# A selective scan with six of sixteen states turned by diagonal matrices, four in-place state buffers, and scans of two channel groups at once

## The reference

```
x = x + mixer(ctx, layernorm(x))      # the gate z is layernorm(x)
x = x + ffn(layernorm(x))
# the mixer's core: for each batch b, channel e (512) and state n (16), over time l (512)
dA[l]    = exp(delta[e, l] * A[e, n])
state[l] = state[l-1] * dA[l] + (delta * u)[e, l] * B[n, l]
y[e, l] += state[l] * C[n, l]         # summed over the 16 states
y = (y + D * u) * silu(z)
```

## Time and profile before

| | |
|---|---|
| median of 3 runs | 699.42 us (696.72 to 703.13) |
| the profiled execution | 699.17 us, span 697.4 us |
| scan stage, first scan to last scan | 159.3 to 487.2 us |
| feed-forward network's first matmul | 494.0 us |
| busy, whole span | PE 553.5, DVE 548.0, ACT 565.9, POOL 490.5 us |

### The profile page before, as it was taken

The page is one execution under the profiler, slowest core; times in us unless marked ns, Lnnn a source line. Parts: engine busy times, 40 slices in busy tenths (PEclk is TensorE's granted clock), DMA queues, the critical chain, the costliest instruction groups (busy, mean ns, idle before and its releaser), DMA issues.

```text
span 697.4 us, 10143 instructions
## 1 busy us (share of the span) xinstructions
PE 553.5 (79%) x3560; PEld 391.0 (56%) x3560; DVE 548.0 (79%) x815; ACT 565.9 (81%) x769; POOL 490.5 (70%) x253
## 2 busy tenths in 40 slices
PE   5877788116897778877897776868889999999975
PEld 2433335116786768776786776866345454545442
DVE  3972262548999999999999999999499898988761
ACT  3873636759999999999999997977378898989773
POOL 2999255006999989999999986889455656555561
PEclk9988657557999999999999998899899999999999
DMA  8900090930121136221722228121300000000000
GB/s 281 361 1 0 0 344 25 382 129 31 48 60 54 53 84 189 61 62 57 207 72 60 59 53 267 47 56 37 60 1 16 31 26 22 30 16 31 16 31 30
DMA packets 25076, 59.16 MB, mean 85 GB/s; under 512 B 5105, under 2 KB 5105, under 8 KB 23362
## 3 DMA queue, kind: packets, MB, share of 16 engines
q1 hardware_dynamic: 22914, 54.32, 22.9%
q0 software_dynamic: 2112, 4.19, 3.5%
HBM read 47.89 MB, written 10.62 MB: 84 GB/s over the span
## 4 chain that ended last, share of the span: by engine, by line
ACT 44%; PE 36%; DVE 8%; POOL 5%; issue 4%; DMA 3%; POOLq 0%; DVEq 0%; SPq 0%; ACTq 0%
ACT arena L506 19%; ACT arena L510 19%; PE ps L942 15%; PE ps L957 6%; ACT arena L453 3%; PE ps L797 3%; PE ps L779 3%; PE ps L885 2%; DVE arena L640 2%; DVE arena L571 2%; POOL arena L321 2%; PE ps L896 2%; PE ps L949 2%; DMA arena<-w_all 1%; DMA arena<-ctx_t 1%
## 5 line engine op out<-in xcount | busy, mean ns | idle before, releaser
L354 POOL TENSOR_TENSOR arena<-arena 128x1024 f32<-128x1024 f32 x128 | 300.4, 2388 | 68.1 <-DVE arena L640 55.4
L640 DVE TENSOR_TENSOR_SCAN arena<-arena,ps 128x512 f32<-128x512 f32 x256 | 290.2, 1199 | 22.1 <-PE ps L885 16.6
L885 PE MATMUL ps<-ident,arena 128*128 128x128 f32 x1024 | 161.8, 283 | 76.0 <-ACT arena L506 63.0
L885 PEld LDWEIGHTS ps<-ident,arena 128*128 128x128 f32 x1024 | 121.3, 145 | 91.0 <-ACT arena L506 68.5
L506 ACT ACTIVATE arena<-arena,bT 128x512 f32<-128x512 f32 x256 | 162.9, 706 | 4.7 <-DMA w_ternary<-arena 4.7
L896 PE MATMUL ps<-ident,arena 128*128 128x128 f32 x1024 | 158.9, 278 | 8.1 <-DVE arena L647 4.7
L510 ACT ACTIVATE arena<-arena,a_neg 128x512 f32<-128x512 f32 x256 | 163.2, 707 | 0.1
L896 PEld LDWEIGHTS ps<-ident,arena 128*128 128x128 f32 x1024 | 123.0, 143 | 11.1 <-POOL arena L354 4.8
L942 PE MATMUL ps<-arena 128*128 128x512 bf16 x512 | 120.9, 386 | 4.8 <-DVE arena L724 2.6
L382 POOL TENSOR_TENSOR arena<-arena 128x1024 f32<-128x1024 f32 x32 | 75.4, 2355 | 26.6 <-DVE arena L724 26.6
L942 PEld LDWEIGHTS ps<-arena 128*128 128x128 bf16 x512 | 49.3, 99 | 61.0 <-issue 8.6
(11 more groups left out here) (90 smaller groups left out, 641.7 us busy)
## 6 DMA issues: line engine op xcount, KB each, us to landing
arena<-c_rows SPq DMA_DIRECT2D x64, 256.0 KB, 3.2
arena<-w_all SPq DMA_DIRECT2D x12, 1024.0 KB, 9.5
w_ternary<-arena SPq DMA_DIRECT2D x12, 512.0 KB, 7.7
arena<-w_ternary SPq DMA_DIRECT2D x3, 2048.0 KB, 10.1
arena<-x SPq DMA_DIRECT2D x4, 1024.0 KB, 8.1
arena<-x POOLq DMA_DIRECT2D x4, 1024.0 KB, 12.4
out<-arena SPq DMA_DIRECT2D x16, 256.0 KB, 2.0
arena<-ctx_t SPq DMA_DIRECT2D x2, 1024.0 KB, 8.5
```

The lines of the kernel that those rows point to most:

```text
L354: nc.gpsimd.tensor_tensor(ps_[:, s, 2 * half:2 * half + 2, :], hs[:, s, 2 * half:2 * half + 2, :], c_bc[:, s:s + 1, :].to_broadcast([P, 2, ...
L640: nc.vector.tensor_tensor_scan(out=hs[:, s, i, :], data0=dA[:, s, i, :], data1=ps[:, 4 + i, :], initial=0.0, op0=ALU.mult, op1=ALU.add).th ...
L885: last = nc.tensor.transpose(ps[:, 4 + i, c * P:(c + 1) * P], dB[:, s, c, i * P:(i + 1) * P], ident[:])
```

## The change

- In states n = 1, 3, 9, 11, 13 and 15 (24 of 64 values of k) ACT no longer scales `turned` into `dB`. It scales the 128x128 identity by the column B[n] into `dgB`, four instructions of 128x128, and TensorE multiplies `turned` itself by this diagonal matrix: four real float32 matmuls of 128x128 for each group instead of four transposes. `dB` and `dgB` have two buffers each, by order of use.
- `hs` has four buffers (`RING`), and the product is written in place over the state; `ps_` is gone. `product(k)` is one instruction of 128x2048 after all of scan k, where it was two of 128x1024.
- A scan covers two groups, 128x1024. The carry from one group to the next is cut by a zero in column 0 of `dA`: one memset before the first scan sets it, and L510's exponentials write columns 1 to 511 only. VectorE waits, as ACT does, until the ternary weights are stored, since `dA` lies over their staging.
- TensorE's stream goes by halves (two groups) and adds one state later; `gate_y` moves from n = 1 to n = 2.
- `xn` and `q1` move, and have one place for the early tiles and one for the later ones.

The diff, cut to what acts in the scan stage:

```diff
+RING = 4
+DIAG = (1, 3, 9, 11, 13, 15)
...
-        hs = part(128, 16).rearrange("p (s k l) -> p s k l", s=2, k=KE)
-        ps_ = part(144, 16).rearrange("p (s k l) -> p s k l", s=2, k=KE)
+        dgB = part(198, 4).rearrange("p (s k e) -> p s k e", s=2, k=KL)
+        hs = part(128, 32).rearrange("p (s k l) -> p s k l", s=RING, k=KE)
         c_bc = part(160, 4).rearrange("p (s l) -> p s l", s=2)
         skip = part(196, 2).rearrange("p (k e) -> p k e", k=KE)
-        q1 = part(198, 3).bitcast(BF16).rearrange("p (s n) -> p s n", s=EARLY)
-        xn = part(201, 2)
+        xn_early = part(72, 2)
+        q1_early = part(74, 3).bitcast(BF16).rearrange("p (s n) -> p s n", s=EARLY)
...
+        def is_diag(k):
+            return k % DS in DIAG
+
+        def slot(k):
+
+            return len([j for j in range(k) if is_diag(j) == is_diag(k)]) % 2
+
+        def slot_free(k):
+
+            same = [j for j in range(k) if is_diag(j) == is_diag(k)]
+            return same[-2] * KE + KE if len(same) > 1 else 0
...
-                hold(sp, "p_ready", (k - 2) * 2 + 2)
+                hold(sp, "p_ready", k - 1)
...
             def product(k):
                 s = k % 2
                 pool.wait_ge(c_loaded[s], (k // 2 + 1) * 16)
-                for half in range(2):
-                    hold(pool, "scan_done", k * KE + 2 * half + 2, *added(k - 2, half))
-                    nc.gpsimd.tensor_tensor(
-                        ps_[:, s, 2 * half:2 * half + 2, :], hs[:, s, 2 * half:2 * half + 2, :],
-                        c_bc[:, s:s + 1, :].to_broadcast([P, 2, L]), ALU.mult).then_inc(S["p_ready"], 1)
+                pool.wait_ge(S["scan_done"], k * 2 + 2)
+                nc.gpsimd.tensor_tensor(hs[:, k % RING, :, :], hs[:, k % RING, :, :],
+                                        c_bc[:, s:s + 1, :].to_broadcast([P, KE, L]),
+                                        ALU.mult).then_inc(S["p_ready"], 1)
...
-                    hold(act, "dBu_ready", (k - 2) * KE + KE)
+                    hold(act, "dBu_ready", slot_free(k))
                     for i in range(KL):
-                        nc.scalar.activation(dB[:, s, i, :], turned[:, b, i, :], ACT.Copy,
-                                             scale=bT[:, b, i, n:n + 1]).then_inc(S["dB_ready"], 1)
+                        if is_diag(k):
+                            nc.scalar.activation(dgB[:, slot(k), i, :], ident[:], ACT.Copy,
+                                                 scale=bT[:, b, i, n:n + 1]).then_inc(S["dB_ready"], 1)
+                        else:
+                            nc.scalar.activation(dB[:, slot(k), i, :], turned[:, b, i, :], ACT.Copy,
+                                                 scale=bT[:, b, i, n:n + 1]).then_inc(S["dB_ready"], 1)
                     for i in range(KE):
-                        hold(act, "scan_done", (k - 2) * KE + i + 1)
-                        nc.scalar.activation(dA[:, s, i, :], delta_u[:, b, 0, i, :], ACT.Exp,
+                        hold(act, "scan_done", (k - 2) * 2 + i // 2 + 1)
+                        nc.scalar.activation(dA[:, s, i, 1:], delta_u[:, b, 0, i, 1:], ACT.Exp,
                                              scale=a_neg[:, i, n:n + 1]).then_inc(S["dA_ready"], 1)
...
             def scan(k):
-                b, s = k // DS, k % 2
-                for i in range(KE):
-                    hold(dve, "p_ready", (k - 2) * 2 + i // 2 + 1)
-                    dve.wait_ge(S["dA_ready"], k * KE + i + 1)
-                    dve.wait_ge(S["dBu_ready"], k * KE + i + 1)
-                    nc.vector.tensor_tensor_scan(out=hs[:, s, i, :], data0=dA[:, s, i, :], data1=ps[:, 4 + i, :],
-                                                 initial=0.0, op0=ALU.mult, op1=ALU.add).then_inc(S["scan_done"], 1)
+                for h in range(2):
+                    two = slice(2 * h, 2 * h + 2)
+                    if k >= RING:
+                        hold(dve, *added(k - RING, h))
+                    dve.wait_ge(S["dA_ready"], k * KE + 2 * h + 2)
+                    dve.wait_ge(S["dBu_ready"], k * KE + 2 * h + 2)
+                    nc.vector.tensor_tensor_scan(out=flat(hs[:, k % RING, two, :]), data0=flat(dA[:, k % 2, two, :]),
+                                                 data1=flat(ps[:, 4 + 2 * h:6 + 2 * h, :]), initial=0.0, op0=ALU.mult,
+                                                 op1=ALU.add).then_inc(S["scan_done"], 1)
 
             def gate_y(b):
...
+            for k in range(4):
+                dve.wait_ge(wq_stored[k], 16 * 3)
+            step(nc.vector.memset(dA[:, :, :, 0], 0.0))
             for b in range(NB):
                 for n in range(DS):
                     scan(b * DS + n)
-                    if b > 0 and n == 1:
+                    if b > 0 and n == 2:
...
             def turn(k, i):
-                s = k % 2
                 pe.wait_ge(S["dB_ready"], k * KL + KL)
-                hold(pe, "scan_done", (k - 1) * KE + i + 1)
+                hold(pe, "scan_done", (k - 1) * 2 + i // 2 + 1)
                 for c in range(KL):
-                    last = nc.tensor.transpose(ps[:, 4 + i, c * P:(c + 1) * P], dB[:, s, c, i * P:(i + 1) * P],
-                                               ident[:])
+                    to = ps[:, 4 + i, c * P:(c + 1) * P]
+                    if is_diag(k):
+                        last = mm(to, turned[:, k // DS, c, i * P:(i + 1) * P], dgB[:, slot(k), c, :], start=True,
+                                  stop=True)
+                    else:
+                        last = nc.tensor.transpose(to, dB[:, slot(k), c, i * P:(i + 1) * P], ident[:])
                 last.then_inc(S["dBu_ready"], 1)
 
             def add(k, i):
 
-                b, n, s = k // DS, k % DS, k % 2
-                pe.wait_ge(S["p_ready"], k * 2 + i // 2 + 1)
+                b, n = k // DS, k % DS
+                pe.wait_ge(S["p_ready"], k + 1)
                 for c in range(KL):
                     if n == 0 and i == 0:
                         hold(pe, "y_gated", (b - 1) * KL + c + 1)
-                    last = mm(ps[:, c, i * P:(i + 1) * P], ps_[:, s, i, c * P:(c + 1) * P], ident[:],
+                    last = mm(ps[:, c, i * P:(i + 1) * P], hs[:, k % RING, i, c * P:(c + 1) * P], ident[:],
                               start=(n == 0 and i == 0), stop=(n == DS - 1), is_transpose=True,
                               skip_group_check=True)
                     if n == DS - 1 and i == KE - 1:
@@ -911,21 +944,26 @@
                 for i in range(KE):
                     turn(k, i)
             for k in range(NB * DS):
-                for i in range(KE):
+                for half in ((0, 1), (2, 3)):
                     if k + 2 <= LAST:
-                        turn(k + 2, i)
-                    add(k, i)
-                    if 4 <= k % DS < 4 + KL:
-                        add_skip(k // DS, i, k % DS - 4)
+                        for i in half:
+                            turn(k + 2, i)
+                    if k > 0:
+                        for i in half:
+                            add(k - 1, i)
+                            if 4 <= (k - 1) % DS < 4 + KL:
+                                add_skip((k - 1) // DS, i, (k - 1) % DS - 4)
+            for i in range(KE):
+                add(LAST, i)
...
```

18 lines of the change are left out of this document (12 added, 6 removed).

## The result

Over 15 runs of each on one chip the changed kernel takes 706.33 us (median; 702.92 to 709.24), the kernel before 696.88 (695.03 to 703.13). The ratio is 1.012, 95% interval [1.010, 1.014]: 1.2% slower, where no change was forecast. The profiled execution took 705.02 us with a span of 703.2, against 699.17 and 697.4.

What follows compares the result with a forecast made beforehand. ACT was taken to bound batches 0 to 2 and VectorE the last, all four engines nearly level. -8.3 + 6.0 + 3.4 = +1.1 on 699.17 us gave 700.3, stated as 700.5 us, range 688 to 711.

Steps and rivals of the forecast that it cites:

- ACT relieved, TensorE and VectorE bind next: Scan stage: ACT falls from 4.90 to 4.33 us a state, leaving TensorE (4.38) and VectorE (4.36) level.
- Wide scan 2.18, one product 4.45 us: Scan stage: a VectorE scan of 1024 takes 2.18 us, a GpSimd product of 128x2048 4.45 us.
- Batches 0 to 2, -8.3 forecast: First three batches: scans 209.3, TensorE 9.6, gates 6.2, cold start 1.6; 226.7 us against 235.0.
- Each such state costs 0.3 us: Diagonal state on TensorE: turn, sums, turn and semaphores take 4.7 us; VectorE could have begun at 4.36.
- The 1.6 us charged for a cold start: First diagonal state after a cold start: half of its turns at half clock, 1.6 us late.
- rival 2: Slower: TensorE's diagonal turns bind every batch, from 0.24 us a matmul on; 708 to 712 us, chance 0.22.
- Rival 1: Faster: TensorE does not bind, states go at GpSimd's 4.45 us; 687 us in all, chance 0.28.
- The last batch, +6.0 forecast: Last batch: three quantising stops of 5.4 us behind GpSimd's longer product, plus TensorE's waits and clock; 98.9 against 92.9 us.
- The tail, +3.4 forecast: Last scans to last gate: whole product after the scans, then 13 transposes; 7.4 us against 4.0.
- the full-clock end of the estimate: Tail: the 13 transposes take 1.4 us at full clock, not 2.8 at half; +2.0 instead of +3.4.
- Feed-forward network, 0 forecast: Feed-forward stage: the same on every engine, so no change.
- an exchange of the binding engine: Whole kernel: what three batches win is paid back in the fourth and the tail; 693 to 706 us, chance 0.47.

Runs made afterwards that it cites:

- e7: Changed kernel, but in the last batch GpSimd starts the product of states 3, 7 and 11 only after VectorE has quantised the tile: 696.73 us.
- e3: Changed kernel with TensorE doing all four turns of state k + 2, then all four sums of state k - 1, instead of alternating by halves: 702.75 us.
- e8: Kernel before with only the six diagonal states added; narrow scans, two buffers and product halves kept: 689.54 us.
- e10: Changed kernel with the in-place product in two halves, scans of 512, and turns and sums by single groups; six diagonals and four buffers kept: 690.12 us.
- e2: Changed kernel with the in-place product in two instructions of 128x1024, each after its half of the scan; sums wait by halves: 691.58 us.
- e6: Kernel before with only the product made one instruction of 128x2048, not in place, two state buffers, no diagonals, scans of 512: 710.79 us.
- e1: Changed kernel without diagonal states, every state turned by transposes; the rest of the change stays: 703.58 us.
- e4: Changed kernel with diagonals in states 1, 3, 13 and 15 only; states 9 and 11 go back to transposes: 699.73 us.

## Why the prediction was wrong

The sum said +1.1 us on the profiled execution, and it was +5.8. The step that failed is the price of a diagonal state on TensorE's path, 0.3 us by the prediction and 0.71 us in the trace. By its own terms:

- **ACT relieved, TensorE and VectorE bind next: right.** The activation of 128 columns takes longer than my line between 64 and 512 columns:

```profile
L528 ACT ACTIVATE arena<-ident,bT 128x128 f32<-128x128 f32 x96 | 30.4, 388 | 0.0
```

  With the overlap of 93 ns it costs 0.295 us, not 0.23. Since ACT then idled, this moved nothing. The estimate from the page that the prediction set beside it (the Trainium skill, "ScalarE: Activation LUTs", What ACT_TABLE_LOAD costs), 0.29 us, is what the trace shows.
- **Wide scan 2.18, one product 4.45 us: right** for the scan (2.18 measured), 2% low for the product (4.54, two in 9.08).
- **Batches 0 to 2, -8.3 forecast, -3.1 measured: this step failed.** The 231.9 us are 96 scans of 2.18 (209.3, as forecast), two gates and TensorE's lateness. The gates took 254.31 - 249.11 = 5.20 and 333.42 - 326.62 = 6.80 us, each less the one scan that ran in between: 3.0 and 4.6, 7.6 against 6.2. The lateness is the remainder, 15.0 us against 9.6 + 1.6. VectorE's timeline around the two gates:

```profile
249.11 2.46 DVE L674 TENSOR_TENSOR arena<-ps,arena 128x512 f32<-128x512 f32 x4
251.48 2.28 DVE L666 TENSOR_TENSOR_SCAN arena<-arena,ps 128x1024 f32<-128x1024 f32 x1
254.31 26.49 DVE L666 TENSOR_TENSOR_SCAN arena<-arena,ps 128x1024 f32<-128x1024 f32 x12 [0.55 <-PE ps L916]
...
326.62 2.46 DVE L674 TENSOR_TENSOR arena<-ps,arena 128x512 f32<-128x512 f32 x4
329.00 2.27 DVE L666 TENSOR_TENSOR_SCAN arena<-arena,ps 128x1024 f32<-128x1024 f32 x1
333.42 26.50 DVE L666 TENSOR_TENSOR_SCAN arena<-arena,ps 128x1024 f32<-128x1024 f32 x12 [2.15 <-PE ps L916]
```

  The failed term is "Each such state costs 0.3 us". The prediction followed the right path, from the end of the scan that frees the first two banks to the second half of the diagonal state: turn, sums, turn. TensorE's rows of it:

```profile
218.87 2.02 PE L916 MATMUL ps<-arena 128*128 128x128 f32 x16 [0.24 <-DVE arena L666]
220.73 1.04 PE L929 MATMUL ps<-ident,arena 128*128 128x128 f32 x8
221.60 1.95 PE L916 MATMUL ps<-arena 128*128 128x128 f32 x16
```

  The scan ends at 216.46 + 2.27 = 218.73 and the waiting one starts at 223.69: 4.96 us, not 4.7. The semaphores take 0.28 us (0.3 charged) and the sums 0.87 (as charged). But the first turn holds TensorE for 220.73 - 218.87 = 1.86 us and the last matmul of the second ends 1.95 us after its start, where both were put at 1.76. And VectorE could have begun 3 x 2.18 - 2.27 = 4.27 us after that end, not 4.36: consecutive scans overlap by 0.09. So the state is 4.96 - 4.27 = 0.69 us late, and the period says 0.71.

  States 13 and 15, and state 1 of batches 1 and 2, cost 0.71 us each. States 9 to 11 cost 3.25 us in batch 0 (the four waits and the lost overlaps) and 2.6 in batches 1 and 2, not 2.0. In these two state 3's second half stands right behind the gate, so its wait is in the gates' 7.6 us; in batch 0 it cost 0.5 us. With the 0.4 us that the first seven scans lost, batch 0 comes to 5.6 us and each of the others to 4.7, against 3.2 charged. The 1.6 us charged for a cold start did not come in this execution, but it did in e7, where the wait is 1.60 us at a clock of 0.50.
- **Why it binds.** The matmul was right (0.22 us: the sixteen records of a half's turn start 1.79 to 1.86 us before the next group). What is short is slack: a wide scan frees two banks at a time, and TensorE then has 4.27 us for 4.96 us of turn, sums and turn. e3 shows that the order within the state is not the main cause. e8 and e10 show that the amount of work is not: by single groups the same matmuls keep VectorE at 1.12 and 1.13 us a scan. This is rival 2 (diagonal turns bind every batch) in effect but not in mechanism, since its condition, 0.24 us a matmul or more, was not met. Rival 1's "TensorE does not bind" all but holds in e8, with narrow scans.
- **The last batch, +6.0 forecast, +8.6 measured.** The mechanism, VectorE's quantising waiting for GpSimd's running instruction, was right in its place and size: stops of 5.4 us forecast, 5.68, 5.43 and 5.42 measured. e2, e6 and e7 show it three ways. What remains of the last batch, 101.5 - 69.8 - 3.9 - 0.3 - 16.5 = 11.0 us, stands for gate, TensorE's lateness and its clock, for which I had 8.7. With halves (e2) it is 3.1 us less, and the granted clock of the batch 0.94; how much of that is the clock and how much the shorter gaps, no run tells.
- **The tail, +3.4 forecast, +2.3 measured.** The product ran whole after the scans, as said, but TensorE had only its 4.53 us of queued transposes and a gap of 2.76 us, and did the last 16 at full clock (1.96 us, granted clock 1.00 from 498 to 500). So the full-clock end of the estimate came, and not the half-clock 2.8 us. It need not have: in e1 and e4, with the same product and the same transposes, TensorE was granted 0.71 and 0.73 there, and the tails are 7.2 and 6.9 us.
- **Feed-forward network, 0 forecast, -2.8 measured.** Its first matmuls met a less throttled TensorE, 15 in 5.08 us at a granted clock of 0.66 (502 to 507), against 16 in 6.45 us at 0.50 (493.7 to 499) before. That is some 1 us. The rest is not explained; over the thirteen other kernels of this document, whose feed-forward code does the same, this stretch took 201.7 to 206.3 us, so 2.8 us may mean nothing. The first scan came 0.7 us later. So the terms' errors add up: +5.2 + 2.6 - 1.1 + 0.7 - 2.8 = +4.6, within rounding the difference between +5.8 and +1.1.
- **What no term could hold:** 3.6 us of the 9.4 between the medians lie in where the two profiled executions stood among their runs. The changed kernel's had full clock at the cold start and behind the first gate, where e7 with the same code had half; 2.4 us hang on that.

The whole went the way of "an exchange of the binding engine", but it was not an even one. Each alone in the kernel before, the long product costs 1.9% (e6, 5.6 us of it in batches 0 to 2, which the changed kernel does not pay) and the diagonals gain 1.1% (e8). In the changed kernel undoing the product gains 2.1% (e2), and undoing the diagonals 0.4% (e1, not clear of the noise): the wide scans took away what the diagonals had to give.

## What to carry to other kernels

When two engines pass buffers back and forth and their work per step is equal, count the slack in steps of the coarser of the two: making scans half as many here saved 0.1 us a state and took away the slack that a heavier step needed. Compare the time from the end of the step that frees a buffer to the start of the one that needs it, and not the sums of work. The length of a GpSimd instruction is also the time for which a VectorE instruction of the kind that waits for it (here TENSOR_SCALAR, not the scan) can stand still; ask what GpSimd has just begun wherever one of these lies on the path. And change one part at a time: one of these parts was worth 1.1% alone, another cost 1.9% alone, and the sum hid both. Before a difference of one stretch between two traces is given a cause, look whether two traces of the same code differ there as much.
